# A state-space layer and its MLP on eight cores: four of a step's sixteen decays as a power on GpSimd

## The reference

```python
delta = jax.nn.softplus(xp[..., -1:] * w_dt + b_dt)
A = -jnp.exp(A_log)                       # per channel and state: -1 .. -16
dA = jnp.exp(delta[..., None] * A)        # the decays
dBx = (delta * xc)[..., None] * B_in[:, :, None, :]
def step(h, inp):
    dA_t, dBx_t, C_t = inp
    h = dA_t * h + dBx_t
    y_t = jnp.einsum('bdn,bn->bd', h, C_t)
    return (h, y_t)
...
y = ys.transpose(1, 0, 2) + D_param * xc
y = y * jax.nn.silu(z)
```

## Time and profile before

| | us |
|---|---|
| median of 3 runs | 3773.28 |
| fastest | 3773.26 |
| the profiled execution | 3764.61 |
| its span on the slowest core (core 7) | 3762.9 |
| spans of the eight cores | 3745.0 to 3762.9 |
| TensorE busy | 3159.1 (84%) |
| VectorE busy | 3081.9 (82%) |
| ScalarE busy | 2804.6 (75%) |
| GpSimd busy | 1072.8 (29%) |

### The profile page before, as it was taken

The page is one execution under the profiler, slowest core; times in us unless marked ns, Lnnn a source line. Parts: engine busy times, 40 slices in busy tenths (PEclk is TensorE's granted clock), DMA queues, the critical chain, the costliest instruction groups (busy, mean ns, idle before and its releaser), DMA issues.

```text
span 3762.9 us, 72464 instructions; the slowest of 8 cores (3745.0 to 3762.9 us)
## 1 busy us (share of the span) xinstructions
PE 3159.1 (84%) x21816; PEld 2076.7 (55%) x21816; DVE 3081.9 (82%) x2688; ACT 2804.6 (75%) x4260; POOL 1072.8 (29%) x1486
## 2 busy tenths in 40 slices
PE   2666668898899898898898998899898998887897
PEld 0233335565566665565566665566565665555676
DVE  0399988798999999998998889998998989898700
ACT  1577766878688887889689887889689787878422
POOL 1311233212342214312342315412342214301122
PEclk9888889999999999999999999999999999999999
DMA  9224895344444454444453454444443444343475
GB/s 138 74 59 68 112 139 147 107 133 127 146 141 127 135 160 135 127 132 127 151 152 117 128 168 142 118 136 140 151 150 114 127 141 141 116 124 110 138 236 193
DMA packets 266006, 500.76 MB, mean 133 GB/s; under 512 B 27536, under 2 KB 60688, under 8 KB 263440
## 3 DMA queue, kind: packets, MB, share of 16 engines
q1 hardware_dynamic: 242192, 423.95, 38.1%
q0 software_dynamic: 6544, 55.27, 9.8%
q10 hardware_dynamic: 16896, 16.91, 1.3%
HBM read 517.60 MB, written 55.18 MB: 152 GB/s over the span
## 4 chain that ended last, share of the span: by engine, by line
PE 42%; DVE 18%; ACT 18%; issue 15%; DMA 4%; POOL 2%; DVEq 1%; ACTq 0%; POOLq 0%; SPq 0%
DVE hq L963 13%; PE ps_f L665 8%; PE ps_f L629 7%; ACT da L808 7%; PE ps_dbx L482 6%; PE ps_f L507 6%; PE ps_y L498 5%; DVE hm L973 5%; ACT L808 3%; DMA wr<-w_scr 2%; ACT hh L868 2%; PE ps_f L518 2%; PE ps_f L571 1%; ACT L868 1%; ACT L749 1%
## 5 line engine op out<-in xcount | busy, mean ns | idle before, releaser
L963 DVE TENSOR_TENSOR_SCAN hq<-da,state,ps_dbx 128x512 bf16<-128x512 f16 x1536 | 1856.1, 1262 | 264.5 <-PE ps_dbx L482 230.9
L808 ACT ACTIVATE da<-delta,prm_sb 128x512 f16<-128x512 f32 x2048 | 1340.8, 713 | 55.3 <-DVE hq L963 43.6
L482 PE MATMUL ps_dbx<-dp,vt 128*128 128x256 bf16 x4096 | 638.7, 281 | 240.6 <-DVE hq L963 236.6
L963 DVE TENSOR_TENSOR_SCAN hq<-da,ps_dbx 128x512 bf16<-128x512 f16 x512 | 586.0, 1199 | 206.3 <-PE ps_dbx L482 205.3
L973 DVE TENSOR_TENSOR hm<-hq,crep 128x2048 bf16<-128x2048 bf16 x512 | 647.5, 1265 | 0.2 <-DVE hq L963 0.2
L482 PEld LDWEIGHTS ps_dbx<-dp,vt 128*128 128x128 bf16 x4096 | 379.2, 100 | 473.2 <-issue 383.8
L507 PE MATMUL ps_f<-xT,wr 128*128 128x512 bf16 x2048 | 510.5, 394 | 79.7 <-DMA wr<-w_scr 63.8
L1081 POOL CAST state<-hq 128x4 f32<-128x4 bf16 x384 | 71.7, 187 | 1759.1 <-DVE hm L973 1759.1
L498 PE MATMUL ps_y<-hm,cst_sb 128*128 128x512 bf16 x2048 | 556.9, 397 | 3.9 <-DVE hm L973 3.9
L629 PE MATMUL ps_f<-y,wr 128*128 128x256 bf16 x4096 | 494.6, 275 | 63.3 <-ACT hh L868 24.1
L629 PEld LDWEIGHTS ps_f<-y,wr 128*128 128x128 bf16 x4096 | 395.7, 98 | 164.6 <-issue 93.7
(11 more groups left out here) (88 smaller groups left out, 2809.4 us busy)
## 6 DMA issues: line engine op xcount, KB each, us to landing
wr<-w_scr SPq DMA_DIRECT2D x1552, 256.0 KB, 3.0
w_scr<-wts POOLq DMA_DIRECT2D x28, 1024.0 KB, 16.0
crep<-c_scr POOLq DMA_DIRECT2D x32, 512.0 KB, 4.3
outT<-rr ACTq DMA_DIRECT2D x16, 1024.0 KB, 6.2
xt_scr<-xt POOLq DMA_DIRECT2D x8, 1024.0 KB, 11.0
xT<-xt_scr SPq DMA_DIRECT2D x8, 1024.0 KB, 6.2
wr<-xt_scr SPq DMA_DIRECT2D x64, 128.0 KB, 3.2
w_scr<-wts POOLq DMA_DIRECT2D x1, 512.0 KB, 54.4
```

The source lines that it names most:

```text
L482: i = t.matmul(ps_dbx[s % 2][:, tb * 256:(tb + 1) * 256], vt[g % 2][:, tb * P:(tb + 1) * P], dp[:, k * 1024 + tb * 256:k * 1024 + (tb + 1) ...
L808: s_.activation(da[:, (e % NDA) * T:(e % NDA + 1) * T], delta[g % 2][:], AF.Exp, scale=a_col(dt, 2 * k + n)).then_inc(s_da, 1)
L963: v.tensor_tensor_scan(hq[:, at:at + T], da[:, (e % NDA) * T:(e % NDA + 1) * T], ps_dbx[s % 2][:, n:2 * T:2], first, OP.mult, OP.add).then ...
```

## The change

ScalarE computes 12 of a step's 16 decays (NA). The other four, states 12 to 15, are computed on GpSimd as a power: exp(A ln(1 + e)) = (1 + e)^A. For that e gets a tile of its own (`edt`, two in turn), ScalarE writes delta from it as before, and GpSimd then adds 1 to e in place (ED, slot 0) and raises it to the power A in four instructions (DAP 0 to 3, slots 1 to 4), into four fp16 tiles `dap`. The exponent is a column of 128 values, broadcast over the 512 tokens as a second input. VectorE's scans of slots 6 and 7 wait for `dap` in place of `da`. ScalarE has no decays in the slots that would compute states 12 to 15. The waits of delta_exp and delta_ln follow the new tiles. To make room in SBUF, four rings are smaller.

```diff
-NXC = 20
-NY = 20
+NXC = 19
+NY = 19
 NZ = 3
-NDA = 11
-NHM = 3
+NDA = 9
+NHM = 2
+NA = 12
@@ plan
         pool[g * NP + 2].append(("DD", g))
+        pool[g * NP].append(("ED", g))
+        for e in range(4):
+            pool[g * NP + 1 + e].append(("DAP", g, e))
@@ scalar_program
             if g >= 2:
-                s_.wait_ge(s_da, 16 * (g - 1))
-            s_.activation(delta[g % 2][:], dtrep[:], AF.Exp, bias=prm[:, C_BDT + dt:C_BDT + dt + 1],
+                s_.wait_ge(s_dap, (NST - NA) * (g - 1))
+            s_.activation(edt[g % 2][:], dtrep[:], AF.Exp, bias=prm[:, C_BDT + dt:C_BDT + dt + 1],
                           scale=prm[:, C_WDT + dt:C_WDT + dt + 1]).then_inc(s_edt, 1)
         def delta_ln(g):
             s_.wait_ge(s_edt, g + 1)
-            s_.activation(delta[g % 2][:], delta[g % 2][:], AF.Ln, bias=1.0).then_inc(s_delta, 1)
+            if g >= 2:
+                s_.wait_ge(s_da, NA * (g - 1))
+            s_.activation(delta[g % 2][:], edt[g % 2][:], AF.Ln, bias=1.0).then_inc(s_delta, 1)
@@ decays
+            if 2 * k >= NA:
+                return
             for n in range(2):
-                e = 2 * s + n
+                e = NA * g + 2 * k + n
                 if e >= NDA:
-                    s_.wait_ge(s_scan, e - NDA + 1)
+                    gp, np_ = divmod(e - NDA, NA)
+                    s_.wait_ge(s_scan, NST * gp + np_ + 1)
@@ scan (VectorE)
-            e = 2 * s + n
-            v.wait_ge(s_da, e + 1)
+            if 2 * k < NA:
+                e = NA * g + 2 * k + n
+                v.wait_ge(s_da, e + 1)
+                decay = da[:, (e % NDA) * T:(e % NDA + 1) * T]
+            else:
+                e = 2 * k + n - NA
+                v.wait_ge(s_dap, (NST - NA) * g + e + 1)
+                decay = dap[:, e * T:(e + 1) * T]
@@ gpsimd_program
+        def exp_delta(it):
+
+            _, g = it
+            p.wait_ge(s_delta, g + 1)
+            p.tensor_scalar(edt[g % 2][:], edt[g % 2][:], 1.0, None, OP.add).then_inc(s_edt1, 1)
+
+        def decay_power(it):
+            _, g, e = it
+            dt = g % NDT
+            p.wait_ge(s_edt1, g + 1)
+            if g > 0:
+                p.wait_ge(s_scan, NST * (g - 1) + NA + e + 1)
+            a = prm[:, C_ALOG + dt * NST + NA + e:C_ALOG + dt * NST + NA + e + 1]
+            p.tensor_tensor(dap[:, e * T:(e + 1) * T], edt[g % 2][:], a.broadcast_to([P, T]),
+                            OP.pow).then_inc(s_dap, 1)
```

More of the change, by code:

```diff
@@ L309, in build_nc @@
     s_delta = nc.alloc_semaphore("s_delta")
+    s_edt1 = nc.alloc_semaphore("s_edt1")
+    s_dap = nc.alloc_semaphore("s_dap")
     s_da = nc.alloc_semaphore("s_da")
@@ L364, in build_nc @@
     delta = [nc.alloc_sbuf_tensor(f"delta{j}", [P, T], F32) for j in range(2)]
+    edt = [nc.alloc_sbuf_tensor(f"edt{j}", [P, T], F32) for j in range(2)]
+    dap = nc.alloc_sbuf_tensor("dap", [P, (NST - NA) * T], FP16)
     vv = nc.alloc_sbuf_tensor("vv", [P, T], BF16)
@@ L962, in scan @@
             at = ((qi % 2) * 4 + st) * T
-            v.tensor_tensor_scan(hq[:, at:at + T], da[:, (e % NDA) * T:(e % NDA + 1) * T],
+            v.tensor_tensor_scan(hq[:, at:at + T], decay,
                                  ps_dbx[s % 2][:, n:2 * T:2], first, OP.mult, OP.add).then_inc(s_scan, 1)
@@ L1166, in gpsimd_program @@
                     conv_diag(it)
+                elif kind == "ED":
+                    exp_delta(it)
+                elif kind == "DAP":
+                    decay_power(it)
                 elif kind == "DD":
```

## The result

The changed kernel takes 43842.46 us (median of 4), against 3773.27 us before: ratio 11.629, 95% interval 11.613 to 11.646. The direction was as forecast; the time is eight times the top of the range (5480 us).

What follows compares the result with a forecast made beforehand. No single bound: TensorE and VectorE full in down-projection steps, ScalarE in up-projection steps. At 4 us a power, 127 steps of 29.95 us plus both ends gave 4208; adding 9, rounded, 4215 us; range 3640 to 5480.

Steps and rivals of the forecast that it cites:

- The price of a power: On GpSimd, one power over 128x512 takes 4 us; lower end 1.15 us, upper end 14 us.
- more than 6.5 us: Upper case of the rival that a power is much dearer and GpSimd is the bound: 5478 us at 6.5; chance 0.18.
- The serial chain: Above 3.5 us a power, GpSimd and VectorE wait for each other in turn across steps: 29.95 us per step at 4 us.
- P: The time of one GpSimd power over 128x512, taken as 4 us.
- the loop: Closed chain through GpSimd's slots and VectorE's scans and hm: 11.15 + 4P, plus 2.8 us other GpSimd work per step.
- The port: A power reads SBUF and holds VectorE's hm for what remains of P; hm's mean rises to 2 us or more.
- ScalarE's relief: Four of 16 exps per step and a table load go; at most 3.5 us per up-projection step, 130 us in all.
- Moved or delayed: In GpSimd's queue, v, cdiag and layer-norm work come later behind powers, halo copies stay ahead of DAP 0; nothing added.
- The rings: Smaller rings (hm 2, decays 9, convolved and gated tiles 19) cost nothing; up to 26 us as a bound.
- Rival 1: A GpSimd power is as cheap as a product (1.15 to 1.5 us), only ScalarE's relief remains: about 3645 us; chance 0.16.

Runs made afterwards that it cites:

- the products: Changed kernel with each power replaced by a product over three of the four tiles, 2.75 us median, scans waiting for all four: 4158 us, ratio 1.1046.
- the fill: The kernel with products over three tiles, each product replaced by a fill of the four tiles with zero, 1.80 us: 3876 us, from one execution.

## Why the prediction was right or wrong

**The price of a power: wrong, and it decides all.** "Upper end: a logarithm, a product and an exponential in software, a dozen arithmetic steps, each a whole pass of 1.15 us: 14 us. I take 4 us". It is 81.9 us, 20 times the value taken and 6 times the upper end. That end was no bound. The nearest rows bound a power from below, since it can't be cheaper than a product; no row limited how long a software routine may run, and counting its steps by the passes of another instruction assumed a routine as lean as those. The chance of 0.18 for "more than 6.5 us" was the right case, and it lay outside the range.

**The serial chain: right.** With the measured price, the prediction's 11.15 + 4P + 2.8 gives 11.15 + 327.7 + 2.8 = 341.7 us per step and 43800 us; measured 338.75 and 43818 (its execution's span). The two hms of 1.2 us in that sum are not paid, since powers leave them alone: 339.3 remain. ED took 1.53 us for the 1.35 estimated. The size of the loop was worked out from rows of before and held to 1%; what failed was one factor in it. That 43800 comes within 20 us of the measured span is luck: the step is 2.95 us shorter than 341.7, 375 us over 127 steps, and the two ends, ahead of the first gate and behind the last, take 585.2 + 211.3 = 796.5 us and not the 404 of before, 393 us more.

**The port: right for products, wrong for powers.** The trace of before showed products holding hm, and the prediction carried this over to an operation it had never seen. A power holds hm for 0.92 us and not for P, and hm's mean is 1335 ns where 2 us or more were expected; most of what it has above 1200 ns comes from 77 hms beside other instructions of GpSimd (median 1.82 us). The Trainium skill's rule ("SBUF — State Buffer", Who interferes with whom) names any GpSimd instruction that reads SBUF; here it agrees with the products (hm 1687 ns) and with the fill (1275 ns), and differs from the powers, which read SBUF and hold hm for 0.92 of 81.9 us only. The measurement decides. Why the port is free for the rest was not settled.

**ScalarE's relief: right in kind, too large.** 130 us forecast, about 72 measured, in the up-projection steps alone, as forecast. ScalarE was relieved by 3.37 us in the step shown and table loads fell by 48 (254 to 206, 40 forecast), but "TensorE's 24.76 us stand behind" took the next engine's busy time for the next bound; a chain over three engines ended the step at 26.98.

**Moved or delayed: wrong.** "The halo copies stay ahead of DAP 0": true, but ED was put ahead of them, and that alone cost some 80 us with products. "The loop covers most, and I add nothing": at 2.9 us a power it is 2.8 us per step, more than the port's share of 1.7 at that length.

**The rings: right,** 1.0015.

**Rival 1: wrong in its time.** Even at a product's price the change as written is 2% slower, 3841 us and not 3645: 48 us of the relief that didn't come (3693 with nothing on GpSimd), and some 150 us for five short instructions in the wrong places of GpSimd's queue. Slower was therefore surer than 0.73: even at the price of a product, the lowest that the prediction allowed, this kernel was not faster.

## What to carry to other kernels

An operation that the trace does not show has a lower bound from its neighbours but no upper one; time it by itself in one instruction before a plan is built on an engine's idle time. Work that is put into an idle engine's queue costs by what stands behind it there: ask first which waits of other engines end on that queue, and put new work behind those, not ahead. And when a bound engine is relieved, expect the chain across engines, not the next engine's busy time, to take its place.

## What the hardware showed that was not expected

- GpSimd's power takes 0.16 us per column and 0.3 us besides, for 1 partition as for 128, for f32 and fp16 output, for bf16 throughout, and for any of the values tried: 81.9 us over 128x512, where a product takes 1.04.
- A power over 128x512 holds VectorE's two-input multiplication for its first 0.92 us and leaves it alone for the 81 us behind (1.20 us inside a power of 82 us); products hold it for their whole length, and are held by it (3.73 us for 2.75); a fill does not hold it.
- GpSimd's addition of a constant over 128x512 f32 took 1.5 us, more than the two-input product of the same size (1.04 us).
- With TensorE busy 9% of the span, its mean granted clock was 0.541, near the lower of its two levels (1.2 of 2.4 GHz), against 0.952 before; 16 matmuls of the up-projection that start some 2.5 us after a wait of 151 us took 2.81 us, where they took 1.91 us in the kernel before. It cost little here: TensorE has 1% of the chain that ended last.
